# Query normalisation of a delta-rule attention kernel moved into the output's root mean square

## The chip, the cores and the metric

The kernel runs on one core of a Trainium2 chip. The metric is the device time of one execution in microseconds (us). TensorE is called PE below, VectorE DVE, ScalarE ACT, GpSimd POOL, SyncE SP.

## What is computed

Input is x of shape (2, 4096, 256). Three layers follow one another, each added to x: a feed-forward layer, a gated delta-rule attention with 16 heads of 16 channels, and the feed-forward layer again. The part that the change touches is the attention:

```
q = silu(dwconv(x @ Wq));  k, v likewise          # per head, 16 channels
q = q * rsqrt(sum(q*q) + 1e-6) * 16 ** -0.5
k = k * rsqrt(sum(k*k) + 1e-6)
for t: S = S * exp(g); S += outer(k, (v - k @ S) * beta); o = q @ S
o = o * rsqrt(mean(o*o) + 1e-5) * norm_w
o = o * silu(gate);  out = o @ Wo
```

The state S does not depend on q, and o is linear in q. A factor on q (it is one number for a head and a time) is therefore a factor on o, and the second root divides by o's own size.

## The kernel before

All data is fp32. A group is 128 times of both batches; there are 32 groups, and one tile of a group holds 128 partitions by 512 columns (COLS). The kernel is a software pipeline, written by hand: every engine runs a Python loop over 38 steps (`GROUPS + 6`), and in a step it calls about 30 to 50 short functions, each for another group (`on(f, c)`: a is the step's own group, b one behind, c two, d three and so on). The order of the calls in that loop is the order on the engine. Engines meet in semaphores alone, one for each product (`s["silu_q"]` and so on), and a wait stands ahead of the instruction that needs it. An instruction that waits holds up all that stands behind it on its engine. PSUM has eight banks of 512 columns, each shared by several products of a step, so that some waits are for a bank and not for data.

What matters for the change, in the order of one group:

- ACT `silu_q` (L783) writes the queries into CV0, `square_q` (L791) squares them into SQ0; PE `q_squares` (L573) sums over a head with one 128x512 matmul against `same_head` into bank 4; ACT `q_root` (L875) makes the inverse root by Ln and Exp; DVE `q_normed` (L1306) multiplies CV0 by it into `KQI[:, 1]`. Keys go the same way (`k_squares` L581, `k_root` L887, `k_normed` L1167), into `KQI[:, 0]`; `KQI[:, 2]` holds a constant.
- PE `gram0` to `gram3` multiply the keys by `KQI`, DVE reads the result, and solves a triangular system (`solve`, tile TZ); `t_turn` (L1138) transposes it into T2. PE `t_product0` and `t_product1` (KP,T) multiply with it, DVE `t_out0` and `t_out1` write WP, PE `d_product0` to `3` (WP,KD) follow, then DVE `d_out0` to `3`.
- PE `o_product` in four parts (QE,S and WP,V) makes o in bank 0; ACT `o_square` (L881) squares it into OSQ; PE `o_squares` (L591, the matmul is L598) sums over a head; ACT `o_root` (L893) makes the inverse root; POOL `gate_norm` (L1009) multiplies it by the gate; DVE `o_norm` (L1191) writes OT; PE `wo` projects it (w_o). Then come PE's `turn2`, `d_product2`, `d_product3` and `k_proj` (w_k), the key projection of a later group.
- POOL `q_decayed` (L1016) multiplies the normalised queries by the decay.

A matmul of fp32 runs in two passes: the trace shows two MATMUL and two LDWEIGHTS records for each that the program has, and the listings of the order below count one.

Of the kernel before, what the change touches and what calls it, by code (L numbers as in the profile page):

```python
# [9 lines left out]
ALU = mybir.AluOpType  # L10
# [4 lines left out]
C = 16  # L15
# [20 lines left out]
def macaron_kernel(nc, x, wts, ffn_mu, convw, wab, hp, consts, blocks, out):  # L36
    with ExitStack() as ctx:
# [12 lines left out]
        normw, eps5, eps6, eps6q = (headp[:, i:i + 1] for i in range(4))  # L50
# [20 lines left out]
        SQ = [sb(f"SQ{i}", [P, COLS]) for i in range(2)]  # L71
        RN = SQ
        KQI = sb("KQI", [P, 3, COLS])
# [42 lines left out]
        def bank(i):  # L116
# [3 lines left out]
                 "q_ps k_ps v_ps g_ps ssk_ps ssq_ps oss_ps wo_ps eq_ps d_ps ea_ps hal1 hal3 haly rstd1 rstd2 rstd3 "  # L120
# [40 lines left out]
        def _(sp_):  # L161
# [32 lines left out]
            put(KQI[:, 2, :], blocks[:, COLS:2 * COLS], s["mix_in"])  # L194
# [6 lines left out]
        def _(pe):  # L201
# [250 lines left out]
            def gram0(g):  # L452
                pe.wait_ge(s["k_slots"], 4 * g + 4)
                pe.wait_ge(s["qhat"], g + 1)
                pe.wait_ge(s["ea"], g + 1)
                for i in range(RING):
                    pk = 0 * RING + i
                    last = pairs(4 * BANK + i * 3 * C, 3 * C, K4, pk, KQI[:, :, pk * C:(pk + 1) * C], start=True, stop=True)
                last.then_inc(s["gram_ps"], 1)

            def gate(g):
                if g == 0:
                    pe.wait_ge(s["mix_in"], 16 * (len(MIX_IN) + 6))
# [11 lines left out]
            def gram1(g):  # L475
                pe.wait_ge(s["k_slots"], 4 * g + 4)
                pe.wait_ge(s["qhat"], g + 1)
# [3 lines left out]
                for i in range(RING):  # L481
                    pk = 1 * RING + i
                    last = pairs(6 * BANK + i * 3 * C, 3 * C, K4, pk, KQI[:, :, pk * C:(pk + 1) * C], start=True, stop=True)
                last.then_inc(s["gram_ps"], 1)

            def gram2(g):
                pe.wait_ge(s["k_slots"], 4 * g + 4)
                pe.wait_ge(s["qhat"], g + 1)
                pe.wait_ge(s["gram_used"], 4 * g + 1)
                for i in range(RING):  # L490
                    pk = 2 * RING + i
                    last = pairs(4 * BANK + i * 3 * C, 3 * C, K4, pk, KQI[:, :, pk * C:(pk + 1) * C], start=True, stop=True)
                last.then_inc(s["gram_ps"], 1)

            def gram3(g):
                pe.wait_ge(s["k_slots"], 4 * g + 4)
                pe.wait_ge(s["qhat"], g + 1)
# [8 lines left out]
                for i in range(RING):  # L506
                    pk = 3 * RING + i
                    last = pairs(3 * BANK + i * 3 * C, 3 * C, K4, pk, KQI[:, :, pk * C:(pk + 1) * C], start=True, stop=True)
# [10 lines left out]
            def ffn3_r(g):  # L519
                pe.wait_ge(s["xr3"], g + 1)  # L520
                pe.wait_ge(s["gram_used"], min(4 * g + 11, 4 * GROUPS))
                if g >= GROUPS - 1:
                    pe.wait_ge(s["wp"], min(2 * g + 4, 2 * GROUPS))
                    pe.wait_ge(s["wp"], min(2 * g + 3, 2 * GROUPS))
                    pe.wait_ge(s["rnq"], min(g + 3, GROUPS))
# [87 lines left out]
            for step in range(0, GROUPS + 6):  # L613
# [40 lines left out]
                on(q_squares, b)  # L654
                on(o_product, d, 3)
                on(k_squares, b)
                on(o_squares, d)
                on(t_product0, c)

        @block.scalar  # L660
        def _(act):
# [45 lines left out]
            def k_slots(g):  # L707
# [3 lines left out]
                in_slots(K4, KQI[:, 0, :], s["k_slots"])  # L711
# [909 lines left out]
```

## Time and profile before

| | us |
|---|---|
| median of three runs | 1972.13 |
| lowest and highest run | 1966.24, 1974.1 |
| span of the profiled execution | 1970.6 |
| PE matmul busy | 1809.7 (92%) |
| DVE busy | 1601.0 (81%) |
| ACT busy | 1034.9 (53%) |
| POOL busy | 414.1 (21%) |
| chain that ended last: PE, DVE, issue | 76%, 10%, 9% |

The profile is one execution, and its times run from its first instruction to its last. A steady step of the pipeline takes some 57 us in it. "Issue" is time in which an engine waited for nothing that the profile shows. Clock is the granted clock of TensorE, 1.00 for 2.4 GHz and 0.50 for 1.2 GHz; a figure between is a mean over the stretch. Busy time of PE is counted from modelled ends of matmuls, so neighbouring records overlap by some 70 ns, and lengths are better read from start to start.

### The profile page before, as it was taken

What the parts mean: (1) busy time and instruction counts of PE and PEld (TensorE: products, weight loads), DVE (VectorE), ACT (ScalarE), POOL (GpSimd) and SP (SyncE); (2) the same over time, 40 slices, a digit from 0 to 9 for tenths busy, and PEclk for the clock granted to TensorE, in tenths of its full rate; (3) what the DMA queues carried; (4) which work ended last, traced back from release to release, by engine and by line L of the source; (5) the groups of instructions that cost most, each with busy time, mean ns of one, the idle gap of its engine ahead of it and who ended that gap; (6) DMA issues with size and microseconds to landing.
All of it is one profiled execution on the core that took longest, in us unless ns stands there. A gap on an engine that the chain in (4) does not pass through costs nothing.

```text
span 1970.6 us, 102023 instructions
## 1 busy us (share of the span) xinstructions
PE 1809.7 (92%) x45376; PEld 1515.8 (77%) x45376; DVE 1601.0 (81%) x4326; ACT 1034.9 (53%) x1999; POOL 414.1 (21%) x325
## 2 busy tenths in 40 slices
PE   4689999999999999999999999999999999998886
PEld 3577787887878787878778877878887887787765
DVE  3777898888888888888988888899888889887631
ACT  3644555555555545555555555555555556554422
POOL 0212122222212222221222222122122221221200
PEclk8878999999999999999999999999999999998766
DMA  3000000000000000000000000000000000000000
GB/s 102 1 3 3 14 14 14 4 14 14 14 14 14 9 9 14 14 14 15 14 5 12 14 14 14 14 14 10 7 14 14 14 9 9 9 4 9 8 8 12
DMA packets 21447, 26.26 MB, mean 13 GB/s; under 512 B 2193, under 2 KB 20753, under 8 KB 21009
## 3 DMA queue, kind: packets, MB, share of 16 engines
q1 hardware_dynamic: 21008, 19.73, 3.0%
q8 instruction: 359, 5.88, 1.2%
q14 instruction: 80, 0.65, 0.1%
HBM read 11.33 MB, written 8.39 MB: 10 GB/s over the span
## 4 chain that ended last, share of the span: by engine, by line
PE 76%; DVE 10%; issue 9%; ACT 1%; DVEq 0%; POOL 0%; ACTq 0%; POOLq 0%
PE ps L239 36%; PE ps L221 15%; PE ps L230 9%; PE ps L214 4%; DVE CV L1107 3%; PE ps L411 2%; PE ps L363 2%; PE ps L589 2%; PE ps L579 2%; PE ps L598 2%; PE ps L207 2%; PE ps L381 1%; DVE XR L1384 1%; DVE eg L1364 1%; PE ps L472 1%
## 5 line engine op out<-in xcount | busy, mean ns | idle before, releaser
L1107 DVE SCALAR_TENSOR_TENSOR CV<-ps,cw,CV 128x256 f32<-128x256 f32 x576 | 250.5, 477 | 8.8 <-ACT CV L872 1.9
L239 PEld LDWEIGHTS ps<-QE,S 64*64 64x64 f32 x4096 | 212.4, 140 | 56.7 <-issue 55.2
L239 PE MATMUL ps<-QE,S 64*64 64x16 f32 x4096 | 254.9, 211 | 1.0 <-ACT S L673 1.0
L239 PE MATMUL ps<-WP,V 64*64 64x16 f32 x4096 | 252.5, 210 | 0.0
L239 PEld LDWEIGHTS ps<-WP,V 64*64 64x64 f32 x4096 | 213.4, 140 | 0.0
L239 PE MATMUL ps<-WP,KD 64*64 64x48 f32 x4096 | 144.6, 226 | 28.6 <-issue 26.8
L239 PEld LDWEIGHTS ps<-WP,KD 64*64 64x64 f32 x4096 | 134.4, 141 | 38.7 <-issue 37.4
L1007 POOL TENSOR_TENSOR XK<-XK 128x512 f32<-128x512 f32 x32 | 33.7, 1052 | 608.5 <-ACT XK L846 608.5
L1122 DVE TENSOR_TENSOR prod<-A,TZ 128x30 f32<-128x30 f32 (+7 forms) x480 | 141.4, 295 | 13.2
L239 PEld LDWEIGHTS ps<-SA,M 32*32 32x32 f32 x8192 | 93.2, 109 | 67.3 <-issue 40.5
L221 PE MATMUL ps<-w_r_ffn,XR 128*128 128x256 f32 x512 | 137.6, 416 | 6.7 <-DVE XR L1096 6.7
L239 PE MATMUL ps<-KQI,K 64*64 64x48 f32 x4096 | 143.4, 223 | 0.3 <-issue 0.3
L239 PE MATMUL ps<-SA,M 32*32 32x16 f32 x8192 | 118.6, 182 | 19.6 <-issue 12.5
L1123 DVE TENSOR_TENSOR TZ<-TZ,prod 128x30 f32<-128x30 f32 (+7 forms) x480 | 122.6, 255 | 16.5
L673 ACT ACTIVATE S<-SA,pair 128x512 f32<-128x512 f32 x128 | 81.9, 710 | 102.0 <-DVE SA L1136 102.0
L221 PE MATMUL ps<-w_v_ffn,XK 128*128 128x256 f32 x512 | 131.1, 399 | 4.6 <-POOL XK L1007 2.0
L239 PEld LDWEIGHTS ps<-KQI,K 64*64 64x64 f32 x4096 | 131.3, 138 | 3.8 <-issue 1.1
L214 PE MATMUL ps<-XK,w_k_ffn 128*128 128x256 f32 x512 | 131.8, 402 | 2.5 <-issue 2.5
L239 PEld LDWEIGHTS ps<-KP,T 32*32 32x32 f32 x8192 | 79.4, 106 | 64.2 <-issue 52.6
L221 PEld LDWEIGHTS ps<-w_r_ffn,XR 128*128 128x128 f32 x512 | 100.7, 207 | 21.3 <-issue 3.8
L239 PE MATMUL ps<-KP,T 32*32 32x32 f32 x8192 | 89.0, 195 | 26.2 <-issue 11.6
L221 PEld LDWEIGHTS ps<-w_v_ffn,XK 128*128 128x128 f32 x512 | 94.0, 194 | 20.3 <-issue 4.8
(156 smaller groups left out, 4019.8 us busy)
## 6 DMA issues: line engine op xcount, KB each, us to landing
X<-in_x SPq DMA_DIRECT2D x32, 256.0 KB, 2.7
out_x<-X SPq DMA_DIRECT2D x32, 256.0 KB, 2.1
w_r_ffn<-in_wT_r_ffn SPq DMA_DIRECT2D x1, 256.0 KB, 3.3
w_k_ffn<-in_wT_k_ffn SPq DMA_DIRECT2D x1, 256.0 KB, 3.6
w_v_ffn<-in_wT_v_ffn SPq DMA_DIRECT2D x1, 256.0 KB, 4.5
w_k<-in_wT_k SPq DMA_DIRECT2D x1, 256.0 KB, 4.5
w_q<-in_wT_q SPq DMA_DIRECT2D x1, 256.0 KB, 4.8
w_v<-in_wT_v SPq DMA_DIRECT2D x1, 256.0 KB, 5.1
```

The lines of the kernel that those rows point to most:

```text
L207: last = nc.tensor.transpose(ps[:, dst * BANK + (k * B + b) * P:dst * BANK + (k * B + b + 1) * P], src[:, b * H + k * P:b * H + (k + 1) * ...
L214: last = mm(ps[:, dst * BANK + m * HB:dst * BANK + (m + 1) * HB], wt[:, k, m * P:(m + 1) * P], src[:, k * HB:(k + 1) * HB], start=(k == 0) ...
L221: last = mm(ps[:, dst * BANK + b * H:dst * BANK + (b + 1) * H], src[:, k * HB + b * TG:k * HB + (b + 1) * TG], wt[:, k, :], start=(k == 0) ...
L230: last = mm(ps[:, o:o + B * (CT + TG)], wt[:, k, m * P:(m + 1) * P], YT[:, k].rearrange("p b t -> p (b t)"), start=(k == 0), stop=(k == M ...
L239: last = mm(ps[rows, o:o + n], stat[rows, pk].rearrange("p s c -> p (s c)"), mov[rows], **flags)
L363: last = mm(ps[:, o:o + P], ST[:, c0:c0 + P], cum_i, start=(ub == 0), stop=False, skip_group_check=True)
L411: last = mm(ps[:, o:o + P], GB[:, c0:c0 + P], cum_i, start=True, stop=True)
L579: mm(bank(4), same_head, SQ[0][:], start=True, stop=True).then_inc(s["ssq_ps"], 1)
L673: af(dst[:, :, i, :], packs(src), ACT.Copy, scale=col).then_inc(signal, 1)
L1107: last = stt(d4[:, m], src, cw[:, i, m, tap:tap + 1], d4[:, m], ALU.mult, ALU.add)
L1122: chained(tt(pr, a_j, t_j, ALU.mult))
L1123: last = tt(t_i, t_i, pr, ALU.subtract)
```

## The change

The queries are no longer scaled. Instead the o that comes out of them is normalised with the epsilon scaled by the same factor: `mean(o*o) + 1e-5 * 16 * (sum(q*q) + 1e-6)`. So `q_squares`, `q_root` and `q_normed` are gone. `silu_q` writes straight into `KQI[:, 1]`, `square_q` carries a scale, and a new POOL addition `o_sum` adds the squares of q to those of o ahead of the head sum of o. KQI has two buffers in place of one and SQ three. On PE `t_product0` now stands ahead of `o_squares`, not behind it. The constant part of KQI is loaded twice.

The core of the diff:

```diff
-        SQ = [sb(f"SQ{i}", [P, COLS]) for i in range(2)]
-        RN = SQ
-        KQI = sb("KQI", [P, 3, COLS])
+        SK = sb("SK", [P, COLS])
+        RK = SK
+        SQ = [sb(f"SQ{i}", [P, COLS]) for i in range(3)]
+        KQI = [sb(f"KQI{i}", [P, 3, COLS]) for i in range(2)]
...
-            put(KQI[:, 2, :], blocks[:, COLS:2 * COLS], s["mix_in"])
+            for i in range(2):
+                put(KQI[i][:, 2, :], blocks[:, COLS:2 * COLS], s["mix_in"])
...
             def gram0(g):
                 pe.wait_ge(s["k_slots"], 4 * g + 4)
-                pe.wait_ge(s["qhat"], g + 1)
+                pe.wait_ge(s["silu_q"], g + 1)
...
-            def q_squares(g):
-                pe.wait_ge(s["sq_q"], g + 1)
...
-                mm(bank(4), same_head, SQ[0][:], start=True, stop=True).then_inc(s["ssq_ps"], 1)
...
             def o_squares(g):
-                pe.wait_ge(s["osq"], g + 1)
+                pe.wait_ge(s["o_sum"], g + 1)
...
             def t_product0(g):
                 pe.wait_ge(s["tp"], g + 1)
-                pe.wait_ge(s["gram_used"], 4 * g + 2)
-                pe.wait_ge(s["rnq"], min(g + 2, GROUPS))
-                if g >= GROUPS - 1:
+                pe.wait_ge(s["gram_used"], 4 * g + 3)
+                if g >= 2:
                     pe.wait_ge(s["th3"], g - 1)
...
                 on(o_product, d, 2)
-                on(q_squares, b)
                 on(o_product, d, 3)
                 on(k_squares, b)
+                on(t_product0, c)
                 on(o_squares, d)
-                on(t_product0, c)
...
             def tap_q(g):
                 act.wait_ge(s["q_ps"], g + 1)
                 if g:
-                    act.wait_ge(s["qhat"], g)
+                    act.wait_ge(s["sq_q"], g)
...
-                af(CV[0][:], CV[0][:], ACT.Silu).then_inc(s["silu_q"], 1)
+                if g >= 2:
+                    act.wait_ge(s["gram_ps"], 4 * g - 4)
+                    act.wait_ge(s["qp"], g - 1)
+                af(KQI[g % 2][:, 1, :], CV[0][:], ACT.Silu).then_inc(s["silu_q"], 1)
...
-                af(SQ[0][:], CV[0][:], ACT.Square).then_inc(s["sq_q"], 1)
+                if g >= 3:
+                    act.wait_ge(s["o_sum"], g - 2)
+                af(SQ[g % 3][:], KQI[g % 2][:, 1, :], ACT.Square, scale=Q_IN_EPS).then_inc(s["sq_q"], 1)
...
-            def q_root(g):
...
-                own.done(af(RN[0][:], bank(4), ACT.Ln, bias=eps6q, scale=float(D)))
-                own.settle()
-                af(RN[0][:], RN[0][:], ACT.Exp, scale=-0.5).then_inc(s["rnq"], 1)
...
-                own.done(af(RO[:], bank(1), ACT.Ln, bias=eps5, scale=1.0 / D))
+                own.done(af(RO[:], bank(1), ACT.Ln, bias=eps_o, scale=1.0 / D))
...
+            def o_sum(g):
+                pool.wait_ge(s["osq"], g + 1)
+                pool.wait_ge(s["sq_q"], g + 1)
+                tt(OSQ[:], OSQ[:], SQ[g % 3][:], ALU.add).then_inc(s["o_sum"], 1)
...
             def q_decayed(g):
                 pool.wait_ge(s["eq"], g + 1)
-                pool.wait_ge(s["qhat"], g + 1)
+                pool.wait_ge(s["silu_q"], g + 1)
...
                 on(square3, g)
+                on(o_sum, f)
                 on(gate_norm, f)
...
-            def q_normed(g):
...
-                tt(KQI[:, 1, :], CV[0][:], RN[0][:], ALU.mult).then_inc(s["qhat"], 1)
...
+EPS_O, EPS_QK = 1e-5, 1e-6
+Q_IN_EPS = D * EPS_O ** 0.5
```

On PE, the end of a steady step and the beginning of the next. Before; SQ is the tile of k's squares, OSQ of o's:

```order
L239 MATMUL ps<-WP,V 64x16 x2
L589 MATMUL ps<-SQ,cst 128x512
L598 MATMUL ps<-OSQ,cst 128x512
L239 MATMUL ps<-KP,T 32x32 x64
L221 MATMUL ps<-w_v_ffn,XK 128x256 x4
L239 MATMUL ps<-KP,T 32x32 x64
L239 MATMUL ps<-WP,KD 64x48 x32
L221 MATMUL ps<-w_o,OT 128x256 x4
```

On PE, the same place now; the tile of k's squares is called SK:

```order
L241 MATMUL ps<-WP,V 64x16 x2
L580 MATMUL ps<-SK,cst 128x512
L241 MATMUL ps<-KP,T 32x32 x64
L589 MATMUL ps<-OSQ,cst 128x512
L223 MATMUL ps<-w_v_ffn,XK 128x256 x4
L241 MATMUL ps<-KP,T 32x32 x64
L241 MATMUL ps<-WP,KD 64x48 x32
L223 MATMUL ps<-w_o,OT 128x256 x4
```

The first 64 of the KP,T matmuls have moved ahead of the sum of o's squares, and that sum now stands between the two halves of KP,T.

On ACT, the same time of the step. Before:

```order
L872 ACTIVATE CV<-ps,cw 128x256 x2
L877 ACTIVATE SQ<-ps,headp 128x512
L879 ACTIVATE SQ<-SQ 128x512
L885 ACTIVATE OSQ<-ps 128x512
L889 ACTIVATE SQ<-ps,headp 128x512
L891 ACTIVATE SQ<-SQ 128x512
L895 ACTIVATE OSQ<-ps,headp 128x512
L897 ACTIVATE OSQ<-OSQ 128x512
```

On ACT, now:

```order
L864 ACTIVATE CV<-ps,cw 128x256 x2
L871 ACTIVATE OSQ<-ps 128x512
L875 ACTIVATE SK<-ps,headp 128x512
L877 ACTIVATE SK<-SK 128x512
L881 ACTIVATE OSQ<-ps,headp 128x512
L883 ACTIVATE OSQ<-OSQ 128x512
```

The two instructions of the query root are gone, and the square of o (OSQ<-ps) stands straight behind the last tap of v.

On POOL, the addition stands ahead of the product of gate and root (GS). Before:

```order
L999 TENSOR_TENSOR GD<-EA,msk 128x512
L1003 TENSOR_TENSOR XK<-XK 128x512
L1007 TENSOR_TENSOR XK<-XK 128x512
L1014 TENSOR_TENSOR GS<-GS,OSQ 128x512
L1023 TENSOR_TENSOR EQ<-KQI,EQ 128x512
```

On POOL, now:

```order
L984 TENSOR_TENSOR GD<-EA,msk 128x512
L988 TENSOR_TENSOR XK<-XK 128x512
L992 TENSOR_TENSOR XK<-XK 128x512
L997 TENSOR_TENSOR OSQ<-OSQ,SQ 128x512
L1004 TENSOR_TENSOR GS<-GS,OSQ 128x512
L1013 TENSOR_TENSOR EQ<-KQI,EQ 128x512
```

One instruction a step has come in on POOL, between the square of the second feed-forward layer (XK) and the gate.

## Rows read from the trace of the kernel before

**Rows 1.** The page: span and part 1.
```profile
span 1970.6 us, 102023 instructions
...
PE 1809.7 (92%) x45376; PEld 1515.8 (77%) x45376; DVE 1601.0 (81%) x4326; ACT 1034.9 (53%) x1999; POOL 414.1 (21%) x325
```

**Rows 2.** Windows, steady stretch: us, busy, instructions, clock, DMA.
```profile
333.30:1767.60 1434.30, 1371.17 (x35451) 1151.18 (x35451) 1254.85 (x3376) 792.00 (x1549) 324.38 (x250) 0.98 0.04 12
```

**Rows 3.** PE timeline, clean step: start, us, engine, line, op, tiles, count, idle.
```profile
1364.50 1.12 PE L579 MATMUL ps<-SQ,cst 128*128 128x512 f32 x2
...
1367.53 1.13 PE L589 MATMUL ps<-SQ,cst 128*128 128x512 f32 x2
...
1368.49 1.02 PE L598 MATMUL ps<-OSQ,cst 128*128 128x512 f32 x2
...
1369.44 1.29 PE L239 MATMUL ps<-KP,T 32*32 32x32 f32 x128
...
1370.66 1.99 PE L221 MATMUL ps<-w_v_ffn,XK 128*128 128x256 f32 x8
...
1373.89 0.66 PE L239 MATMUL ps<-KP,T 32*32 32x32 f32 x53 [0.47 <-issue]
...
1376.47 1.99 PE L221 MATMUL ps<-w_o,OT 128*128 128x256 f32 x8
...
1381.28 2.01 PE L230 MATMUL ps<-YT,w_k 128*128 128x262 f32 x8
```

**Rows 4.** PE and DVE timelines, a step with a long stall.
```profile
400.44 2.04 PE L239 MATMUL ps<-WP,KD 64*64 64x48 f32 x34 [1.76 <-issue]
...
402.41 2.79 PE L221 MATMUL ps<-w_o,OT 128*128 128x256 f32 x8
...
407.56 0.71 PE L230 MATMUL ps<-YT,w_k 128*128 128x262 f32 x2
...
404.37 0.42 DVE L1264 TENSOR_TENSOR M<-GI,ps 128x256 f32<-128x256 f32 x1
```

**Rows 5.** Groups by line and form, PE, 333 to 1768 us.
```profile
L239 PE MATMUL ps<-WP,KD 64*64 64x48 f32 x3200 | 109.9, 223 | 21.7 <-issue 20.1 <-DVE M L1237 1.4
...
L239 PE MATMUL ps<-KP,T 32*32 32x32 f32 x6400 | 68.5, 193 | 9.2 <-issue 8.7
```

**Rows 6.** DMA queues on the page: packets, MB, share.
```profile
q8 instruction: 359, 5.88, 1.2%
```

**Rows 7.** Windows of 4 us after a stall, two steps.
```profile
400.10:404.10 4.00, 3.65 (x38) 3.30 (x39) 3.83 (x15) 1.66 (x3) 0.18 (x1) 0.57 0.40 135
...
632.00:636.00 4.00, 2.85 (x32) 2.47 (x28) 3.86 (x15) 1.09 (x2) 0.00 (x0) 1.00 0.20 68
```

**Rows 8.** ACT timeline, the clean step.
```profile
1367.64 0.60 ACT L885 ACTIVATE OSQ<-ps 128x512 f32<-128x512 f32 x1 [0.63 <-PE ps L239]
...
1369.95 0.67 ACT L895 ACTIVATE OSQ<-ps,headp 128x512 f32<-128x512 f32 x1
```

**Rows 9.** POOL timeline, the clean step.
```profile
1371.35 1.28 POOL L1014 TENSOR_TENSOR GS<-GS,OSQ 128x512 f32<-128x512 f32 x1 [6.99 <-ACT OSQ L897]
...
1372.58 1.72 POOL L1023 TENSOR_TENSOR EQ<-KQI,EQ 128x512 f32<-128x512 f32 x1
```

**Rows 10.** DVE timeline, the clean step.
```profile
1365.19 2.00 DVE L1142 STREAM_TRANSPOSE T<-TZ 128x1024 f32<-128x1024 f32 x1
...
1367.04 2.66 DVE L1107 SCALAR_TENSOR_TENSOR CV<-ps,cw,CV 128x256 f32<-128x256 f32 x6
...
1375.60 0.74 DVE L1195 SCALAR_TENSOR_TENSOR OT<-ps,headp,GS 128x512 f32<-128x512 f32 x1
...
1380.77 0.41 DVE L1264 TENSOR_TENSOR M<-GI,ps 128x256 f32<-128x256 f32 x1
```

**Rows 11.** DVE and POOL at the same time, an earlier step.
```profile
935.35 2.69 DVE L1107 SCALAR_TENSOR_TENSOR CV<-ps,cw,CV 128x256 f32<-128x256 f32 x6
...
935.08 1.27 POOL L1040 TENSOR_TENSOR E<-E,msk 128x512 f32<-128x512 f32 x1 [10.56 <-ACT E L747]
```

More of the change, by code:

```diff
@@ L49, in macaron_kernel @@
         headp = sb("headp", [P, 4 + 2 * BH])
-        normw, eps5, eps6, eps6q = (headp[:, i:i + 1] for i in range(4))
+        normw, eps5, eps6, eps_o = (headp[:, i:i + 1] for i in range(4))
         a_log, dt_b = headp[:, 4:4 + BH], headp[:, 4 + BH:4 + 2 * BH]
@@ L457, in gram0 @@
                     pk = 0 * RING + i
-                    last = pairs(4 * BANK + i * 3 * C, 3 * C, K4, pk, KQI[:, :, pk * C:(pk + 1) * C], start=True, stop=True)
+                    last = pairs(4 * BANK + i * 3 * C, 3 * C, K4, pk, KQI[g % 2][:, :, pk * C:(pk + 1) * C], start=True, stop=True)
                 last.then_inc(s["gram_ps"], 1)
@@ L482, in gram1 @@
                     pk = 1 * RING + i
-                    last = pairs(6 * BANK + i * 3 * C, 3 * C, K4, pk, KQI[:, :, pk * C:(pk + 1) * C], start=True, stop=True)
+                    last = pairs(6 * BANK + i * 3 * C, 3 * C, K4, pk, KQI[g % 2][:, :, pk * C:(pk + 1) * C], start=True, stop=True)
                 last.then_inc(s["gram_ps"], 1)
@@ L491, in gram2 @@
                     pk = 2 * RING + i
-                    last = pairs(4 * BANK + i * 3 * C, 3 * C, K4, pk, KQI[:, :, pk * C:(pk + 1) * C], start=True, stop=True)
+                    last = pairs(4 * BANK + i * 3 * C, 3 * C, K4, pk, KQI[g % 2][:, :, pk * C:(pk + 1) * C], start=True, stop=True)
                 last.then_inc(s["gram_ps"], 1)
@@ L507, in gram3 @@
                     pk = 3 * RING + i
-                    last = pairs(3 * BANK + i * 3 * C, 3 * C, K4, pk, KQI[:, :, pk * C:(pk + 1) * C], start=True, stop=True)
+                    last = pairs(3 * BANK + i * 3 * C, 3 * C, K4, pk, KQI[g % 2][:, :, pk * C:(pk + 1) * C], start=True, stop=True)
                 last.then_inc(s["gram_ps"], 1)
@@ L710, in k_slots @@
                     act.wait_ge(s["gram_ps"], 4 * g)
-                in_slots(K4, KQI[:, 0, :], s["k_slots"])
+                in_slots(K4, KQI[g % 2][:, 0, :], s["k_slots"])
             def rstd3(g):
@@ L832, in square_k @@
                     act.wait_ge(s["khat"], g)
-                af(SQ[1][:], CV[1][:], ACT.Square).then_inc(s["sq_k"], 1)
+                af(SK[:], CV[1][:], ACT.Square).then_inc(s["sq_k"], 1)
             def halo3(g):
@@ L888, in k_root @@
                 act.wait_ge(s["ssk_ps"], g + 1)
-                own.done(af(RN[1][:], bank(6), ACT.Ln, bias=eps6))
+                own.done(af(RK[:], bank(6), ACT.Ln, bias=eps6))
                 own.settle()
-                af(RN[1][:], RN[1][:], ACT.Exp, scale=-0.5).then_inc(s["rnk"], 1)
+                af(RK[:], RK[:], ACT.Exp, scale=-0.5).then_inc(s["rnk"], 1)
             def o_root(g):
                 act.wait_ge(s["oss_ps"], g + 1)
-                own.done(af(RO[:], bank(1), ACT.Ln, bias=eps5, scale=1.0 / D))
+                own.done(af(RO[:], bank(1), ACT.Ln, bias=eps_o, scale=1.0 / D))
                 own.settle()
@@ L972, in _ @@
                 on(tap_v, c)
-                on(q_root, c)
                 on(o_square, e)
@@ L1022, in q_decayed @@
                     pool.wait_ge(s["mt"], 4 * g)
-                tt(QP[:], KQI[:, 1, :], EQ[:], ALU.mult).then_inc(s["qp"], 1)
+                tt(QP[:], KQI[g % 2][:, 1, :], EQ[:], ALU.mult).then_inc(s["qp"], 1)
             def stat1(g):
@@ L1169, in k_normed @@
                 ve.wait_ge(s["silu_k"], g + 1)
-                if g:
-                    ve.wait_ge(s["k_slots"], 4 * g)
-                    ve.wait_ge(s["gram_ps"], 4 * g)
-                tt(KQI[:, 0, :], CV[1][:], RN[1][:], ALU.mult).then_inc(s["khat"], 1)
+                if g >= 2:
+                    ve.wait_ge(s["k_slots"], 4 * g - 4)
+                    ve.wait_ge(s["gram_ps"], 4 * g - 4)
+                tt(KQI[g % 2][:, 0, :], CV[1][:], RK[:], ALU.mult).then_inc(s["khat"], 1)
             def soft_one(g):
@@ L1544, in _ @@
                 on(x2, f)
-                on(q_normed, d)
                 on(stats3, f)
@@ L1602 @@
     arrays["headp"] = np.ascontiguousarray(np.concatenate([
[L1603 removed]
+        np.tile(a["L0_attn_norm_w"], HP)[:, None], np.full((P, 1), 1e-5), np.full((P, 1), 1e-6), np.full((P, 1), EPS_O * D * EPS_QK),
         np.tile(a["L0_attn_A_log"], (P, B)), np.tile(a["L0_attn_dt_bias"], (P, B))], 1).astype(np.float32))
```

36 lines of the change are left out of this document (10 added, 26 removed), and 4 rows, old and new, of the table names.

## The prediction

> **What bounds the kernel now.** I read the page first: PE is busy 92% of 1970.6 us, DVE 81% [rows 1]. That makes PE the suspect, but 8% is idle and DVE is near. So next the windows: from 333 to 1768 us POOL, which issues ten instructions a step, issued 250, so 25 steps took 1434.3 us, 57.4 us each; PE was busy 1371.2 of it, and the clock was 0.98 [rows 2], which is 0.02 x 2 x 1434 = 57 us at half clock. PE idles (1434.3 - 1371.2) / 25 = 2.5 us a step. The groups tell where: 9.2 us ahead of KP,T and 21.7 us ahead of WP,KD matmuls, nearly all of it "issue" [rows 5]. That is 30.9 / 25 = 1.24 us a step in one short stretch, from the T product to w_o.
>
> The long idle pieces there are instruction refills. Queue q8 moved 5.88 MB in 359 packets [rows 6], 16 KB each, and PE has 2 x 45376 records [rows 1]: 64 bytes an instruction, 256 a packet. In 1.22 us of KP,T (1369.44 to 1370.66) PE takes in 256 of them [rows 3], and a second such block follows with only the 1.92 us of w_v between them. In the step of [rows 4] the stall is 1.76 us. Where it falls drifts, since a step is not a whole number of packets.
>
> Then the two step pictures. In the clean step, whose one stall of 0.47 us costs little, PE goes by DVE and not by itself [rows 3]: OT is done at 1375.60 + 0.74 = 1376.34 and w_o starts at 1376.47; the product of L1264 ends at 1380.77 + 0.41 = 1381.18 and w_k starts at 1381.28, 0.10 later [rows 3, 10]. In the stalled step L1264 ends at 404.37 + 0.42 = 404.79, PE comes 2.8 us late (407.56), and w_o takes 2.79 us instead of 1.99 [rows 3, 4] because the clock fell: 0.57 in those 4 us. It need not fall: after a stall of 1.15 us in another step it stayed 1.00 [rows 7]. Over the 25 steps w_k starts 0.10 us after L1264 in seven, up to 1.0 in eight more, and 2.3 to 4.4 us after it in ten, those with the clock down; the mean is 1.39. **So PE is the bound by 1.3 us a step, and DVE is the floor right below it.**
>
> **The change, part by part.** Times are those of the clean step.
>
> q_squares goes: one 128x512 matmul, 1.12 us by its record; the like matmul of k takes 0.96 to the start of the next [rows 3]. I take 1.05, between them. It lies on PE's path, so o_product ends at 1366.48 instead of 1367.53.
>
> k_squares then ends at 1367.44. t_product0 follows and needs T, ready at 1365.19 + 2.00 = 1367.19 [rows 10]: 0.25 us in hand, so nothing. It ends at 1367.44 + 1.22 = 1368.66. In a few steps T may be up to 0.35 us later: 0.1 us, in which o_squares is queued behind it.
>
> o_sum is new, on the path from o's square to its root. ACT squared o at 1367.64, 0.11 after PE's last o matmul [rows 3, 8]; with q_root gone ACT is free, and it starts at 1366.59 and ends at 1367.19. POOL is idle for 7 us there [rows 9]. Its price has no row. The nearest is GS x OSQ, two tiles in and one out of the same size: 1.28 us; the ends are 1.27 for a mask product [rows 11] and 1.72 for EQ [rows 9]. I take 1.28: done at 1368.5 to 1368.6, so it hides behind t_product0. At 1.72 PE waits 0.35 us. A gain below nothing can be excluded: it is an added instruction.
>
> o_squares ends its 0.95 us at 1369.61 instead of 1369.44, later by 0.17, but t_product0 is behind PE already. w_v (ffn3_v) needs the v convolution, which ends at 1367.04 + 2.66 = 1369.70 [rows 10], so it starts at 1369.77, against 1370.66: 0.9 us earlier, and 0.15 of the 1.05 is lost to DVE.
>
> The DVE side moves less. o_root started at 1369.95 behind k_root's Exp [rows 8]; now it starts with o_squares' result, about 1369.71. Then gate_norm and q_decayed on POOL (1371.35 to 1374.30 [rows 9]), with DVE's next products beside them, and OT and L1264 move by the same 0.24 at most, by 0 if DVE's own queue holds them. **DVE's floor comes down by 0.1 to 0.24 us**; I take 0.2.
>
> q_normed (a 128x512 product on DVE) and q_root (two on ACT, as k_root) go from engines that wait at that time; I count nothing, since DVE has a wait for PE behind q_normed. If that cover were gone, some 0.7 us of DVE would count as well.
>
> The refill stalls: w_v starts 0.9 us earlier, so PE reaches w_o at about 1375.1 without a stall (1376.47, less the 0.47 stall at 1373.89 [rows 3], less 0.9), and DVE releases w_o at 1376.2. That is 1.1 us of slack, and the slack up to w_k is 0.9 us more. A stall as in [rows 4], 1.76 us, now mostly lies inside a wait. The two blocks of KP,T also have 2.9 us between them, not 1.92, since o_squares now stands there too. So I take the lateness of w_k behind L1264 to go from 1.39 to 0.1 us in steps without a fall of the clock.
>
> The Trainium skill, "Runtime: NRT & Kernel Launch", section "Instruction fetch mechanics", says that instructions come in 16 KiB blocks of 256 and that the cost of crossing one is "mostly hidden". The trace agrees on the block and not on "hidden", with 1.76 us in one stall. By that rule the idle pieces would have another cause.
>
> **The clock.** PE will idle 1.1 to 1.3 us ahead of w_o in nearly every step, as a wait where it was a stall. In the old trace the clock fell after twelve of the 15 longest stalls of the whole stretch (the one in [rows 4] is among them) and after two of the next ten (the one of 1.15 us [rows 7] is one of the eight). I take a fall in 3 of 10 steps, against ten of 25 now. One costs 4 x (1 - 0.57) = 1.7 us [rows 7], less some slack, 1.3 us at w_k: 0.4 us a step. Ends: none, and in every step 1.3.
>
> The second load of KQI's constant part stands last in SP's queue of loads, which all come before the first projection of the keys. PE waits for it once; I count nothing, against some microseconds once if it came late.
>
> **Sum.** A step gains 1.29 + 0.2 - 0.4 = 1.1 us. Some 28 steps run in this regime: 31 us. The first steps save a q_squares each, the last two or three, which wait for one chain, pay o_sum's 1.3 us each in turn: I count them against one another. Against the profiled span, 1970.6 - 31 = 1939.6; the median of the runs is 1.5 us above the span, so **1941 us**.
>
> **The rivals.**
> 1. *The clock falls in every step*, because the wait ahead of w_o comes every time. Then the gain is 1.29 + 0.2 - 1.3 = 0.2 a step, 6 us: 1966. For it: the idle time is now regular. Against it: two of ten.
> 2. *Refill is a bound of its own.* If packets come at a fixed pace through the whole dense stretch, the microsecond from q_squares is given back as longer stalls. Then only DVE's 0.2 is left: 1966 too. Against it: seven steps without lateness.
> 3. *POOL and DVE block each other.* o_sum (1367.2 to 1368.5) runs beside the v convolution. If that grew by 0.6 us, all up to w_k would be later by it: 1941 + 28 x 0.6 = 1958. Against it: the same six products took 2.69 us beside POOL's mask product and 2.66 without [rows 10, 11]. The Trainium skill, "SBUF — State Buffer", section "Who interferes with whom", gives the rule behind it: a DVE instruction with two SBUF inputs contends with a GpSimd one, one with a single SBUF input does not, and the convolution reads PSUM and one SBUF tile.
> 4. *Slower: the root of o becomes the late chain.* Each 0.1 us of o_sum above 1.5 pushes OT, w_o and w_k by as much in all 28 steps. The gain is used up at 1.5 + 1.1 = 2.6 us. At 3.0 us it is 1972 + 28 x 0.4 = 1983. Nothing of this size on POOL took over 1.72.
> 5. *More than forecast*: no falls of the clock there at all and 0.24 from DVE: 28 x 1.53 = 43 us, 1929; with fewer falls elsewhere 1922.
>
> **Chances.** Forecast (1930 to 1955) 0.60; rival 1 0.12; rival 2 0.08; rival 3 0.08; rival 4 0.04; rival 5 0.08. A measurement of this kernel can tell about 0.5%, 10 us. Forecast, rivals 3 and 5 and the better part of 1 are faster by more: 0.80. The rest of 1 and most of 2: 0.15. Rival 4 and a bad case of 1: 0.05. The range leaves out rivals 1 and 2 above 1962 and the best of 5: 1924 to 1962.
>
> **What would show it.** Right: no idle piece of "issue" that delays w_o, w_o starting some 0.1 us after OT in nearly every step, w_k 0.1 us after L1264's product, o_sum at 1.3 us, o_squares without a wait over 0.2 us, a step of about 56.2 us, and a clock above 0.98. Wrong: w_k still 1 us late on average (rival 2), a clock of 0.96 (rival 1), a longer convolution (3), or PE waiting for o_sum (4).

## The result and the profile after

The kernel before takes 1973.12 us (median of four runs, 1966.24 to 1977.78), the changed one 1951.64 us (four runs, 1944.14 to 1960.12). The ratio is 0.990, with a 95% interval of 0.987 to 0.993. The forecast was 1941 us in a range of 1924 to 1962: the direction holds, and of the 31 us that were expected 21 came. The profiled execution of after took 1944.14 us, 1.8 above its span; it is the lowest of its four runs. The ratios, here and below, leave out three slow runs that the medians contain: two of e12's ten, and one of 3282 us of the kernel before, beside e10 to e13.

The page of the kernel after, to be read against [rows 1] and [rows 6] (q8 is the queue that carries instructions):

```profile
span 1942.3 us, 101795 instructions
...
PE 1788.6 (92%) x45312; PEld 1509.9 (78%) x45312; DVE 1555.4 (80%) x4294; ACT 993.6 (51%) x1935; POOL 454.4 (23%) x357
...
q8 instruction: 358, 5.87, 1.2%
```

PE has 64 records fewer (32 matmuls in two passes), POOL 32 instructions more, and DVE and ACT lost theirs. PE's busy time fell by 21 us of the span, not by the 32 x 1.05 = 34 that the removed matmuls took.

The next view is the windows, with the columns of [rows 2]: the same 25 steps of the kernel after, from the fourth sum of o's squares on.

```profile
326.80:1750.30 1423.50, 1360.70 (x35415) 1151.99 (x35402) 1216.78 (x3351) 760.08 (x1500) 356.64 (x275) 0.96 0.04 12
```

A step takes 56.94 us, not 57.37: 0.43 less, where 1.1 was forecast. PE is busy 1360.7 us, 10.5 less than before, though 25 matmuls of 1.05 us have gone; its idle time is the same (62.8 us, 63.1 before). So the missing part is in the busy time, and the last columns name it: the clock is 0.96, not 0.98. By the clock's own records it was at its lower level for 109 us of these steps, against 58 before.

Where does it fall? The timeline of PE after, in a step where it does. `QE,S` and `WP,V` are the four parts of o_product; the last columns are count and, in brackets, the idle time ahead.

```profile
1231.20 1.99 PE L216 MATMUL ps<-XK,w_k_ffn 128*128 128x256 f32 x8
1233.12 0.29 PE L241 MATMUL ps<-QE,S 64*64 64x16 f32 x4
1233.26 0.27 PE L241 MATMUL ps<-WP,V 64*64 64x16 f32 x4
...
1236.76 0.27 PE L241 MATMUL ps<-WP,V 64*64 64x16 f32 x4
1236.96 1.99 PE L580 MATMUL ps<-SK,cst 128*128 128x512 f32 x2
1238.88 1.85 PE L241 MATMUL ps<-KP,T 32*32 32x32 f32 x128
1240.66 1.13 PE L589 MATMUL ps<-OSQ,cst 128*128 128x512 f32 x2
...
1246.98 0.43 PE L241 MATMUL ps<-WP,KD 64*64 64x48 f32 x8 [0.48 <-issue]
1247.34 1.99 PE L223 MATMUL ps<-w_o,OT 128*128 128x256 f32 x8
1249.17 0.60 PE L209 MATMUL ps<-cst,XN 128*128 128x128 f32 x4
...
1251.70 2.04 PE L232 MATMUL ps<-YT,w_k 128*128 128x262 f32 x8
```

And another step of the same kernel where it doesn't:

```profile
1522.61 1.12 PE L580 MATMUL ps<-SK,cst 128*128 128x512 f32 x2
...
1523.66 1.29 PE L241 MATMUL ps<-KP,T 32*32 32x32 f32 x128
...
1524.88 1.13 PE L589 MATMUL ps<-OSQ,cst 128*128 128x512 f32 x2
...
1526.07 1.97 PE L223 MATMUL ps<-w_v_ffn,XK 128*128 128x256 f32 x8
...
1532.52 1.99 PE L223 MATMUL ps<-w_o,OT 128*128 128x256 f32 x8
...
1537.40 2.01 PE L232 MATMUL ps<-YT,w_k 128*128 128x262 f32 x8
```

From the sum of k's squares to that of o's PE takes 1240.66 - 1236.96 = 3.70 us in the first and 1524.88 - 1522.61 = 2.27 in the second. The windows confirm that this is the clock (the column behind the last bracket): from o_product's start up to k's squares, behind it, and the same 3.5 us of the second step.

```profile
1225.30:1237.00 11.70, 11.70 (x274) 10.60 (x273) 10.74 (x35) 4.28 (x10) 1.05 (x1) 1.00 0.01 3
1237.00:1240.50 3.50, 3.50 (x125) 2.00 (x126) 3.43 (x8) 1.91 (x3) 1.26 (x1) 0.51 0.00 0
1522.60:1526.10 3.50, 3.44 (x137) 1.83 (x133) 3.43 (x8) 1.98 (x4) 1.27 (x1) 1.00 0.02 5
```

PE was busy 11.70 of the 11.70 us ahead of the fall. Such a fall, 10.5 to 12.4 us behind the start of o_product, comes in 14 of the 25 steps after, and in none of the 14 had PE an idle piece since o_product began; before it came in no step. What stood there before was q_squares, a long matmul between o_product 2 and 3. The falls in the stretch of T and w_o, the ones that the prediction spoke of, went the other way: ten before, three after. A third kind, 35 to 39 us behind the start of o_product, came four times before and comes seven times after. Of the 109 us at the lower level 58 belong to the first kind, 17 to the second and 34 to the third (before: 0, 37 and 21). Each fall of the second and third kind, before and after, came while PE was idle or at most 2 us behind an idle piece, with 0.5 to 2.2 us of idle time in it ahead of the fall; the first kind alone came with none.

The second thing is on DVE and POOL. The timeline of both after, first in the step without the fall, then in the one with it. L1133 is the transposition of T, L1098 the v convolution, L1164 `k_normed` (a product of the next keys, two SBUF inputs), L1171 a 128x64 step of the decay, L1186 OT, L1255 the product that w_k waits for; POOL's L997 is o_sum, L1004 gate_norm, L1013 q_decayed.

```profile
1521.41 1.97 DVE L1133 STREAM_TRANSPOSE T<-TZ 128x1024 f32<-128x1024 f32 x1
1523.28 2.64 DVE L1098 SCALAR_TENSOR_TENSOR CV<-ps,cw,CV 128x256 f32<-128x256 f32 x6
1523.40 1.27 POOL L997 TENSOR_TENSOR OSQ<-OSQ,SQ 128x512 f32<-128x512 f32 x1 [2.81 <-ACT OSQ L871]
1527.47 1.28 POOL L1004 TENSOR_TENSOR GS<-GS,OSQ 128x512 f32<-128x512 f32 x1 [2.80 <-ACT OSQ L883]
1527.73 1.57 DVE L1164 TENSOR_TENSOR KQI<-CV,SK 128x512 f32<-128x512 f32 x1
1528.70 1.73 POOL L1013 TENSOR_TENSOR EQ<-KQI,EQ 128x512 f32<-128x512 f32 x1
1529.22 1.26 DVE L1171 TENSOR_SCALAR uz<-nz 128x64 f32<-128x64 f32 x1
1531.72 0.74 DVE L1186 SCALAR_TENSOR_TENSOR OT<-ps,headp,GS 128x512 f32<-128x512 f32 x1
1536.88 0.41 DVE L1255 TENSOR_TENSOR M<-GI,ps 128x256 f32<-128x256 f32 x1
```

```profile
1242.10 0.68 DVE L1164 TENSOR_TENSOR KQI<-CV,SK 128x512 f32<-128x512 f32 x1
1242.70 0.19 DVE L1171 TENSOR_SCALAR uz<-nz 128x64 f32<-128x64 f32 x1
1243.25 1.28 POOL L1004 TENSOR_TENSOR GS<-GS,OSQ 128x512 f32<-128x512 f32 x1 [4.23 <-ACT OSQ L883]
...
1245.00 0.74 DVE L1186 SCALAR_TENSOR_TENSOR OT<-ps,headp,GS 128x512 f32<-128x512 f32 x1
1250.73 0.41 DVE L1255 TENSOR_TENSOR M<-GI,ps 128x256 f32<-128x256 f32 x1
```

The same two DVE instructions take 1.57 + 1.26 us beside POOL's two and 0.68 + 0.19 when they are done before POOL starts: 1.96 us. OT is finished 7.58 us behind the start of o_squares in the first step and 5.08 in the second. Before, the first picture held in every step (7.85 us), as the DVE groups of the kernel before say, with mean 1454 and 1256 ns:

```profile
L1173 DVE TENSOR_TENSOR KQI<-CV,SQ 128x512 f32<-128x512 f32 x25 | 36.3, 1454 | 0.0
L1180 DVE TENSOR_SCALAR uz<-nz 128x64 f32<-128x64 f32 x25 | 31.4, 1256 | 0.0
```

After, both kinds of step occur, and their lengths show why the clock's fall looks harmless there: counted from o_product to o_product, the 14 steps with a fall take 56.94 us on average and the 11 without 56.93. In eight of those 11 gate_norm starts first and both DVE instructions are blocked, as in the first view, where w_k waits for DVE (1536.88 + 0.41 = 1537.29, PE at 1537.40); in two more only the short one is blocked, in one neither. Where the clock falls, o_squares and with them gate_norm come late, DVE slips through in all 14 steps, and in the step shown PE is the late one (1251.14 against 1251.70).

### The profile page after: what moved, and what is told of

It reads as the page before. It is cut to its first block, busy times and chain, and to the rows that moved or that the text cites. A ratio compares the mean times of both kernels' runs of the same rounds, so it can differ in the third digit from the quotient of the medians.

```text
span 1942.3 us, 101795 instructions
## 1 busy us (share of the span) xinstructions
PE 1788.6 (92%) x45312; PEld 1509.9 (78%) x45312; DVE 1555.4 (80%) x4294; ACT 993.6 (51%) x1935; POOL 454.4 (23%) x357
## 4 chain that ended last, share of the span: by engine, by line
PE 74%; issue 13%; DVE 9%; POOL 1%; ACT 1%; DVEq 0%; POOLq 0%; ACTq 0%
PE ps L241 35%; PE ps L223 14%; PE ps L232 9%; PE ps L216 3%; DVE CV L1098 3%; PE ps L580 2%; PE ps L411 2%; PE ps L589 2%; PE ps L363 2%; PE ps L209 1%; PE ps L381 1%; DVE XR L1367 1%; DVE eg L1347 1%; PE ps L472 1%; DVE XK L1087 1%
## 5 line engine op out<-in xcount | busy, mean ns | idle before, releaser
L1098 DVE SCALAR_TENSOR_TENSOR CV<-ps,cw,CV 128x256 f32<-128x256 f32 x576 | 250.4, 476 | 8.8 <-ACT CV L864 2.0
L241 PEld LDWEIGHTS ps<-WP,KD 64*64 64x64 f32 x4096 | 134.7, 141 | 31.6 <-issue 28.3
L241 PEld LDWEIGHTS ps<-KP,T 32*32 32x32 f32 x8192 | 87.9, 117 | 69.3 <-issue 41.2
L241 PE MATMUL ps<-KP,T 32*32 32x32 f32 x8192 | 96.3, 206 | 22.2 <-DVE T L1133 11.1
```

Source lines behind the costliest of these rows:

```text
L241: last = mm(ps[rows, o:o + n], stat[rows, pk].rearrange("p s c -> p (s c)"), mov[rows], **flags)
L1098: last = stt(d4[:, m], src, cw[:, i, m, tap:tap + 1], d4[:, m], ALU.mult, ALU.add)
```

## The experiments

Ratios are to the kernel before on the same chip, with 95% intervals; its median was 1975.65 us beside the first four, 1969.92 beside the next four and 1979.44 beside the last four. "Falls" are falls of the clock behind o_product in 25 steady steps of the profiled execution; "step" is their mean length, from o_product to o_product.

| kernel | us | ratio | falls | step |
|---|---|---|---|---|
| before | | 1 | 0 | 57.37 |
| after | 1951.64 | 0.990 (0.987 to 0.993) | 14 | 56.93 |
| e1_q_sum_unread | 1945.03 | 0.987 (0.981 to 0.994) | 0 | 56.64 |
| e2_v_split | 1929.5 | 0.977 (0.973 to 0.981) | 0 | 56.04 |
| e3_before_q_sum_moved | 2013.49 | 1.022 (1.016 to 1.028) | 16 | 59.04 |
| e4_old_T_order | 2001.65 | 1.013 (1.008 to 1.018) | 15 | 58.81 |
| e5_before_T_ahead | 1952.98 | 0.990 (0.987 to 0.993) | 0 | 57.08 |
| e7_v_split_no_o_sum | 1932.58 | 0.979 (0.976 to 0.983) | 0 | 56.19 |
| e8_before_gate_late | 1972.19 | 1.001 (0.998 to 1.003) | 0 | 57.71 |
| e9_v_split_spare_product | 1925.87 | 0.976 (0.973 to 0.979) | 0 | 55.86 |
| e10_v_split_again | 1930.45 | 0.977 (0.972 to 0.982) | 0 | 56.24 |
| e11_v_split_q_sum | 1953.95 | 0.988 (0.981 to 0.995) | 0 | 56.80 |
| e12_before_v_split | 1971.45 | 0.994 (0.991 to 0.997) | 0 | 57.51 |
| e13_before_split_T_ahead | 1942.5 | 0.983 (0.978 to 0.987) | 0 | 56.63 |

e2 and e10 are the same program; their profiled steps differ by 0.2 us, so smaller differences of one profile say nothing.

### Is it the missing long matmul that lets the clock fall?

**e1**: the changed kernel with the matmul of q_squares back in its place.

```diff
                 on(o_product, d, 2)
+                on(q_squares, b)
                 on(o_product, d, 3)
```

> The changed kernel with the matmul over q's squares put back on PE between o_product 2 and 3. Nobody reads its result, so it only costs PE time; everything else is as changed. Theory A (sparse stretch): in the changed kernel the clock falls at 50 to 55 us of a step, with no idle time ahead of it, because o_product 2 and 3, matmuls of 16 columns, now follow one another with no long matmul between. Then the falls there vanish (14 of 25 steps now, at most 2 here), the clock over the span is 0.945 or more against 0.931, and the time is about that of the changed kernel: 1.05 us a step more work (29 us) against 14 x 1.5 us or so of falls given back: 1950 to 1962. Theory B (the clock falls because of idle time or the phase of the refills, wherever that stands): the falls stay, clock 0.93, time 1951 + 29 = 1980.

It has no fall behind o_product, and it is not slower than the kernel without the matmul. The windows of its 25 steps, and then the DVE groups in them:

```profile
331.40:1747.60 1416.20, 1358.04 (x35465) 1143.12 (x35452) 1206.12 (x3351) 759.55 (x1500) 355.98 (x275) 0.99 0.04 12
```

```profile
L1173 DVE TENSOR_TENSOR KQI<-CV,SK 128x512 f32<-128x512 f32 x25 | 17.0, 681 | 0.0
L1180 DVE TENSOR_SCALAR uz<-nz 128x64 f32<-128x64 f32 x25 | 5.7, 230 | 0.0
```

PE is busy 2.7 us less than in the kernel after, with 25 matmuls more: the clock is 0.99 and not 0.96. But the matmul takes away two things at once. With it o_squares starts 15.1 us behind the start of o_product, and not 13.95 as in the blocked steps of after; so gate_norm comes behind k_normed in every step, and k_normed is blocked in none, where it was in eight of 25. What e1 shows is the price of both together.

**e3**: the kernel before, with q_squares moved behind o_product 3. No work is taken away or added.

```diff
                 on(o_product, d, 2)
-                on(q_squares, b)
                 on(o_product, d, 3)
+                on(q_squares, b)
                 on(k_squares, b)
```

> The kernel before with its matmul over q's squares moved from between o_product 2 and 3 to behind 3. Same work. Theory A: the falls at the end of a step appear in the kernel before as well, clock 0.93 against 0.944, and the time rises by 12 to 25 us, to 1985 to 1998. Theory B: no falls there; the query root comes 2 us later on ACT, which has room, so 1970 to 1980.

It costs more than expected, 2.2%. Sixteen of the 25 steps now have the fall, none with an idle piece of PE since o_product began, and the windows of one show it at the same place:

```profile
1147.20:1158.30 11.10, 11.10 (x257) 10.02 (x258) 10.14 (x35) 4.27 (x10) 1.04 (x1) 1.00 0.01 3
1158.30:1161.80 3.50, 3.50 (x25) 2.12 (x24) 3.43 (x7) 0.41 (x1) 0.00 (x0) 0.50 0.00 0
```

So the order alone brings the fall: two parts of o_product back to back with no long matmul between them. Why nine steps of the same order are spared isn't shown.

The 2.2% is more than the fall. The nine steps without it take 58.45 us on average, against 57.37 before, and PE now waits for ACT's square of o. The group of o_squares in e3 and then in before:

```profile
L598 PE MATMUL ps<-OSQ,cst 128*128 128x512 f32 x51 | 34.3, 758 | 14.9 <-ACT OSQ L885 14.9
L598 PE MATMUL ps<-OSQ,cst 128*128 128x512 f32 x50 | 25.5, 592 | 0.0
```

**e2**: if so, any long matmul will do. In the changed kernel the v projection is cut in halves, and PE runs o_product 0, half of v, o_product 1, half of v, o_product 2, ffn3_k, o_product 3.

```diff
                 on(o_product, d, 0)
                 on(v_proj, b)
                 on(o_product, d, 1)
-                on(ffn3_k, e)
+                on(v_proj1, b)
                 on(o_product, d, 2)
+                on(ffn3_k, e)
                 on(o_product, d, 3)
```

> The changed kernel with its v projection cut in two halves of four matmul records: one half between o_product 0 and 1, as now, the other between 1 and 2, and the k product of the second feed-forward layer between 2 and 3. Same work, no two parts of o_product next to one another. Theory A: the falls at the end of the step vanish and nothing is added: 1951 - 20 = 1925 to 1938, clock 0.945 or more. Theory B: as the changed kernel, 1945 to 1958, clock 0.93.

1929.5 us, faster than before by 2.3% where the change gives 1.0%, with the work of the change. It beats both kernels. The falls behind o_product are gone. The windows of its 25 steps, and then the DVE groups in them:

```profile
324.70:1725.70 1401.00, 1338.00 (x35416) 1134.76 (x35403) 1187.62 (x3352) 759.97 (x1500) 356.05 (x275) 0.99 0.04 12
```

```profile
L1168 DVE TENSOR_TENSOR KQI<-CV,SK 128x512 f32<-128x512 f32 x25 | 17.0, 681 | 0.0
L1175 DVE TENSOR_SCALAR uz<-nz 128x64 f32<-128x64 f32 x25 | 5.7, 229 | 0.0
```

PE's busy time falls by 22.7 us against the kernel after, and POOL blocks k_normed in no step and the short instruction in one. That the second comes with the first wasn't forced; it wasn't isolated why DVE stays ahead here. What the trace shows is that PE, not DVE, is late at w_k, by 1.54 us on average.

**e12**: the split alone, on the kernel before, as a control. q_squares stay where they were.

```diff
                 on(o_product, d, 1)
-                on(ffn3_k, e)
+                on(v_proj1, b)
                 on(o_product, d, 2)
+                on(ffn3_k, e)
                 on(q_squares, b)
```

> The kernel before with its v projection in halves and nothing else: o_product 0, half of v, o_product 1, half of v, o_product 2, ffn3_k, q_squares, o_product 3. If splitting helps only by keeping up the clock, which doesn't fall there in before: no change, 1963 to 1978. Rival, the split is worth something in itself (the squares of k and the v convolution are released earlier or later): 1945 to 1962, or 1980 to 1995.

The median of 1971.45 lies in the first reading, but the ratio of 0.994 leaves a small gain of 0.3 to 0.9%, 6 to 18 us. This control says less than it seems to: DVE is still blocked in it (1.46 and 1.21 us on average), so it can't tell the falls from the block. And a part of what e2 gains over the change may be the split's own: it gives 0.6% here and 0.7% from e5 to e13, which have no fall behind o_product either, and nothing from e1 to e11, with uncertainties of 0.3 to 1.0%. The whole step from the change to e2 is 1.3%.

### What is the other order worth, T product ahead of the sum?

**e4**: the changed kernel with t_product0 behind o_squares, as it was.

```diff
-                on(t_product0, c)
                 on(o_squares, d)
+                on(t_product0, c)
```

> The changed kernel with t_product0 behind o_squares again, as before. PE then waits for the addition on POOL: o_product's end + 0.1 + 0.6 (square) + 0.07 + 1.28 (sum) + 0.06 = 2.1 us, less 0.96 of k_squares: 1.15 us of idle time in each step. Theory 1 (the move pays): some of it lies in the slack ahead of w_o, but the two blocks of KP,T are 1.92 us apart again and refill stalls delay w_o as before: 1965 to 1980. Theory 2 (the slack covers it): 1945 to 1956, and the move of the T product is worth nothing.

Slower than before, by 1.3%, and worse than expected: without this move the change would have been a loss. The group of o_squares in its 25 steps shows the direct part, a wait for POOL of 18.3 us or 0.73 a step:

```profile
L589 PE MATMUL ps<-OSQ,cst 128*128 128x512 f32 x51 | 42.3, 922 | 18.6 <-POOL OSQ L997 18.3
```

Much of the rest is the clock: there are 15 falls behind o_product (six of them in that wait or just behind it, nine with PE busy since o_product began), 11 come in the stretch of T and w_o and 9 later, 164 us at the lower level in all, against 109 after.

**e5**: the other way round, the kernel before with this move alone.

```diff
                 on(k_squares, b)
+                on(t_product0, c)
                 on(o_squares, d)
-                on(t_product0, c)
```

> The kernel before with one part of the change alone: t_product0 stands ahead of o_squares, and q_squares, q_root and q_normed stay. Theory A, the order pays in itself (a longer distance between the two KP,T blocks, w_v later against the v convolution): faster than before by 8 to 25 us, 1950 to 1965. Rival, the order pays only as a cover for o_sum's 1.27 us, which this kernel doesn't have: o_squares and with it the root of o come 1.22 us later, gate_norm 0.7 us later, OT not at all or by up to 0.7 us, so 1973 to 1990.

1952.98 us, ratio 0.990: as much as the whole change gives. The reading of a mere cover for o_sum falls, since this kernel has none. The groups of DVE in its 25 steps show what it gains instead:

```profile
L1173 DVE TENSOR_TENSOR KQI<-CV,SQ 128x512 f32<-128x512 f32 x25 | 17.0, 680 | 0.0
L1180 DVE TENSOR_SCALAR uz<-nz 128x64 f32<-128x64 f32 x25 | 6.9, 274 | 0.0
```

o_squares and gate_norm come 1.2 us later, and the two DVE instructions now finish ahead of gate_norm: 1.75 us less on DVE in each step. OT ends 5.18 us behind the start of o_squares instead of 7.85, so 1.45 us earlier in the step although its root starts later. In the profile, the slowest of its four runs, the steady steps give 0.29 us each of that; PE is now the late one at w_k, by 1.75 us on average. That the unblocked DVE is what gives the 1% wasn't isolated: the two halves of KP,T are also further apart.

**e8**: is it POOL that holds them up? The kernel before with ACT's taps of v ahead of the root of o, so that only gate_norm and q_decayed come later.

```diff
-                on(o_root, e)
                 on(v_slots, d)
+                on(o_root, e)
```

> The kernel before with ACT's v_slots ahead of o_root: POOL's gate_norm and q_decayed start some 2.5 us later, and nothing else is moved. Theory, the two DVE products that run beside them in before (k_normed 1.47 us, the product of L1174 1.25 us) are held up by POOL: they fall to about 0.69 and 0.19 us and DVE's work up to OT shrinks, though OT itself may then wait for gate_norm. OT up to 1 us earlier: 1945 to 1973. Rival, those two are long by themselves: they keep 1.47 and 1.25, and OT comes up to 1 us later: 1973 to 2000.

Yes: with POOL late they take 0.68 and 0.23 us. But OT then waits for gate_norm, 25.5 us in 25 steps, and little is left (OT at 7.66 us, not 7.85); the time doesn't change.

```profile
L1173 DVE TENSOR_TENSOR KQI<-CV,SQ 128x512 f32<-128x512 f32 x25 | 17.0, 681 | 0.0
L1180 DVE TENSOR_SCALAR uz<-nz 128x64 f32<-128x64 f32 x25 | 5.7, 230 | 0.0
L1195 DVE SCALAR_TENSOR_TENSOR OT<-ps,headp,GS 128x512 f32<-128x512 f32 x25 | 18.7, 749 | 25.5 <-POOL GS L1014 25.5
```

### What are the parts on q worth?

All of these stand on e2, where the clock holds.

**e10**: e2 once more, to have it on the chip of the next.

> The kernel of e2_v_split once more, so that the next ones stand beside it on one chip: 1924 to 1936.

1930.45 us.

**e11**: the matmul of q_squares back in.

```diff
                 on(ffn3_k, e)
+                on(q_squares, b)
                 on(o_product, d, 3)
```

> The kernel of e2_v_split with the matmul of q_squares back between o_product 2 and 3, result unread. It asks what one 128x512 matmul on PE is worth once no fall of the clock comes with its absence. Theory of the prediction, PE is the bound and counts 0.95 to 1.05 us a step: plus 27 to 30 us, 1952 to 1962. Rival, instruction refills set the pace (the matmul is two instructions of 2871, and its time lies beside the next packet): plus 0 to 12, 1925 to 1943.

Plus 23.5 us beside the same kernel without it (e10; the intervals of the two ratios just overlap, 0.972 to 0.982 and 0.981 to 0.995). That is 0.84 us in each of 28 steps, near the 0.95 to 1.05 of its record. There is a second reading: e1 has the matmul too and differs from e2 by it and the split, on one chip, and there it is 15.5 us, 0.55 a step. **Where the clock holds and DVE isn't blocked, PE's matmul is worth half its length or more**; refills don't swallow it whole.

**e9**: a spare 128x512 product on DVE at q_normed's place.

```diff
                 on(x2, f)
+                on(spare, d)
                 on(stats3, f)
```

> The kernel of e2_v_split with a spare 128x512 product on DVE at q_normed's place; its result is not used. It measures what taking q_normed away was worth, which the prediction counted as nothing. If DVE has a wait there: within 7 us of e2_v_split, 1923 to 1936. If DVE is the bound there: plus 0.7 us a step or more, 1948 to 1960.

No cost: 1925.87. Its group shows that it ran, 0.68 us each:

```profile
L1304 DVE TENSOR_TENSOR DM<-DM 128x512 f32<-128x512 f32 x25 | 17.1, 683 | 0.0
```

**e7**: no o_sum; the squares of q are left out of the root of o.

```diff
-                on(o_sum, f)
                 on(gate_norm, f)
```

> The kernel of e2_v_split without o_sum: the squares of q are left out of the root of o. This is what POOL's addition costs in all. Theory, it is hidden behind t_product0: within 7 us of e2_v_split, 1923 to 1936. Rival, it costs through DVE, whose v convolution runs beside it (its products would be shorter by 0.3 us or more together), or through PE's wait: 1905 to 1920.

No cost to be seen here either: 1932.58 against 1929.5. The products of the convolutions on DVE average 478 ns with it and without it.

**e13**: the kernel before with both orders, the edits of e5 and e12; the queries are still normalised.

> Everything of e2_v_split but the change on q: before with the v projection in halves and t_product0 ahead of o_squares. Its distance to e2_v_split is what the folding of the queries' scale is worth once the clock holds. From e5_before_T_ahead (1953) by no gain of the split: 1945 to 1960, so the folding would be worth 20 to 28 us. Rival, the two orders are all of the gain and the folding is worth nothing: 1925 to 1938.

1942.5 us, between the two readings. By the medians the folding of the scale is worth 12 us once both orders are right (1930.45 on the same chip), but the intervals of the two ratios overlap (0.978 to 0.987 and 0.972 to 0.982), so that it is worth anything isn't clear of the scatter. PE's matmul alone gave 23.5. Since o_sum and q_normed each show no cost by e7 and e9, the 11 us between the two are open; q_root's two instructions on ACT had no run of their own, e11 scattered most (1939.54 to 1967.61), and no row tells the rest from the scatter.

## Why the prediction was right, and where not

**PE is the bound, with DVE right below**: right, and more delicate than stated. After, w_k starts 0.10 us behind L1255's product in 11 of 25 steps, 0.85 late on average (1.39 before), not nearly always at 0.1 as forecast.

**q_squares, 1.05 us on PE**: the price is right or somewhat high (e11: 0.84, e1 against e2: 0.55), but in the changed kernel it was not collected. The step that failed is the one that says "It lies on PE's path, so o_product ends at 1366.48 instead of 1367.53". It counted the matmul's length and not what its place did for the clock and for DVE. A fall costs 3.70 - 2.27 = 1.43 us at the spot; 14 in 25 steps would be 0.80 a step. That sum doesn't reach the end of the step, though: where the clock holds, DVE is mostly blocked by POOL for 1.96 us, and the two kinds of step are equally long. e1 and e3 show that the order makes the falls; e1 and e2 have neither these falls nor the block of k_normed: e1 is no slower than the changed kernel with the matmul's work added (0.987 against 0.990), and e2 is 1.3% faster without it. How that divides between falls, block and split isn't shown.

**The clock** in the forecast was a fall in 3 of 10 steps, in the T and w_o stretch, after idle time. There it was 3 of 25, so better than forecast. The error was to look for falls behind idle pieces only. Nothing in the trace of the kernel before pointed to others: each of its 14 falls in these steps came during or just behind an idle piece. Rival 1 had the clock as the culprit but at the wrong place and for the wrong reason; its sign, a clock of 0.96, is what the trace shows. The Trainium skill, "TensorE: Matmul & The Clock Gate", section "HAM oscillation — how this bites in real kernels", ties the falls to waits of the matmuls for data; for the falls behind o_product the trace doesn't agree, with 11.70 of 11.70 us busy ahead of the one shown.

**o_sum, 1.28 us, hidden behind t_product0**: right on both. It took 1.27, PE never waited for it (0.0 idle ahead of o_squares in the groups), and e7 finds no cost clear of the scatter. e4 shows the price of the cover gone, 0.73 us a step as a wait and more by the clock.

**w_v 0.9 us earlier, 0.15 of it lost to DVE**: right for a step where the clock holds. The v convolution ended at 1523.28 + 2.64 = 1525.92 and w_v started at 1526.07, 1.19 us behind o_squares.

**"DVE's floor comes down by 0.1 to 0.24 us"**: mis-sized, and here the term hid the larger effect. k_normed and the product behind it were blocked by POOL in every step before, 1.45 + 1.26 us where 0.68 + 0.2 is their length, and that was in the trace to be read. In the eight steps of after in which both are blocked the floor moved by 7.85 - 7.58 = 0.27, as forecast. In the steps with a fall it moved by up to 2.8 less the lateness of o_squares. Rival 3 had POOL and DVE block each other, but with o_sum against the convolution; that pair doesn't (2.64 us beside o_sum). The Trainium skill, "SBUF — State Buffer", section "Who interferes with whom", says that the order of issue decides which of two contending instructions is blocked. The trace agrees for k_normed: 1.57 us when gate_norm began 0.26 us ahead, 0.68 when it began behind.

**The sum** of 1.1 us a step was 0.43, less than half. That the time still lay in the range is luck, and comes of a term counted as zero, "I count them against one another": in the two profiles, 28.3 us apart (the one of after is the lowest of its four runs), the steady steps gave 10.9 and the first and last parts 17.4, 6.5 at the start and 10.9 at the end. The twins e2 and e10 differ by 5 and 6 us in these two parts, so much of it may be scatter; its cause wasn't looked for.

**Rival 2**, refill as a bound of its own: e11 speaks against it (0.84 us a step for the matmul, with the intervals just overlapping). The refill stalls themselves stay: "issue" ahead of the WP,KD matmuls is still 18.8 us in the 25 steps (20.1 before, [rows 5]):

```profile
L241 PE MATMUL ps<-WP,KD 64*64 64x48 f32 x3200 | 110.3, 223 | 19.5 <-issue 18.8 <-DVE M L1228 0.7
```

**Rival 4**: nothing of it; the root of o was never late for o_sum. **Rival 5** named 1929 us, and e2 reaches that number, but not for its reason: six falls in the T and w_o stretch remain in e2, and DVE is no longer blocked.

## What to carry to other kernels

Before a matmul is taken out, look at what stands on both sides of it and at what the other engines do while it runs: here putting a long one back, with its work, cost nothing, since the falls of the clock and the block of DVE went with it, and another long one moved to its place was faster still (a part of that may be the split's own). Read an engine's own products for two lengths of the same instruction (0.68 and 1.57 us here): the difference is another engine's, and shifting one of them by a microsecond may be worth as much as removing work (e5; e8 removed the block and gained nothing, as OT then waited for POOL). Test the reordering that comes with an arithmetic change by itself; here it alone gave the 1% that the whole change gave, and the arithmetic's own gain was never clear of the scatter.

## What the runs showed of the hardware

TensorE's clock fell to its lower level (1.2 GHz) with PE busy without a break, after 11.70 us in one step and 11.10 in another. It fell at this place in 14, 16 and 15 of 25 steps of the three kernels in which o_product 2 and 3 are neighbours (after, e3 and e4), PE having been busy since o_product began in all but six of the 45, all six in e4, and in none of the eleven others, where a long matmul stands between them.

A DVE product with two SBUF inputs went from 0.68 to 1.57 us, and a 128x64 instruction with one from 0.19 to 1.26, when POOL's 128x512 product had started first. With POOL's product late (e8) they took 0.68 and 0.23 us.
